# Turning the 784 tokens of two normalisations in 7 groups of 112 rows instead of 8 groups of 98

## The reference

```python
residual = x
f = _ln(x.transpose(0, 2, 3, 1), g1, b1)          # layer norm over the 96 channels
f = jnp.roll(f, (-3, -3), axis=(1, 2))
win = _window_partition(f)                        # (B * 64, 49, 96)
q, k, v = ...(win @ w_qkv + b_qkv)
attn = softmax(q @ k.T * scale + mask)            # per window and head, 49 x 49
out = (attn @ v) @ w_proj + b_proj
f = residual + roll(_window_reverse(out), (3, 3))
m = _ln(f.transpose(0, 2, 3, 1), g2, b2)          # the second layer norm
m = gelu(m @ w_fc1 + b_fc1, approximate=False) @ w_fc2 + b_fc2
return f + m.transpose(0, 3, 1, 2)
```

## Time and profile before

| what | value |
|---|---|
| median of 3 runs | 3063.34 us |
| the profiled execution, its own time | 3062.91 us |
| its span, first to last instruction | 3061.1 us |
| PE busy with matmuls | 2862.6 us, 94% |
| PE busy with weight loads (PEld, beside the matmuls) | 2299.2 us, 75% |
| DVE busy | 2424.3 us, 79% |
| ACT busy | 2076.6 us, 68% |
| POOL busy | 1454.5 us, 48% |
| mean granted TensorE clock | 0.992 |

### The profile page before, as it was taken

How to read it: one execution, slowest core, us unless ns; L and a number is a source line. 1 busy time by engine, 2 the same in 40 slices (tenths; PEclk the granted TensorE clock), 3 DMA queues, 4 the chain that set the end, 5 groups by cost and what they waited for, 6 DMA issues and landing times.

```text
span 3061.1 us, 137479 instructions
## 1 busy us (share of the span) xinstructions
PE 2862.6 (94%) x53060; PEld 2299.2 (75%) x53060; DVE 2424.3 (79%) x7208; ACT 2076.6 (68%) x3208; POOL 1454.5 (48%) x1832
## 2 busy tenths in 40 slices
PE   1799999999999999999999999999999999999997
PEld 0677777777777777777777777777777777777775
DVE  5778888788887888788787888878888788888885
ACT  0467767667776767767766767767767667777674
POOL 2554454454444444444444454444454454445444
PEclk9899999999999999999999999999999999999999
DMA  1444444444444444444444444444444444444441
GB/s 29 108 119 123 124 125 119 119 126 122 126 127 113 123 123 122 126 121 120 124 126 114 125 124 120 124 123 120 123 125 118 120 126 121 126 127 119 125 113 42
DMA packets 414727, 359.37 MB, mean 117 GB/s; under 512 B 63455, under 2 KB 413985, under 8 KB 414012
## 3 DMA queue, kind: packets, MB, share of 16 engines
q1 hardware_dynamic: 414028, 350.01, 43.7%
HBM read 193.25 MB, written 154.14 MB: 113 GB/s over the span
## 4 chain that ended last, share of the span: by engine, by line
PE 87%; issue 5%; ACT 5%; DVE 2%; POOL 1%; SPq 0%; DMA 0%; POOLq 0%; DVEq 0%; ACTq 0%
PE psum L446 18%; PE psum L379 16%; PE psum L559 11%; PE psum L430 10%; PE psum L414 8%; PE psum L472 7%; PE psum L487 6%; PE psum L532 5%; ACT probs L618 4%; PE psum L522 3%; PE psum L395 2%; PE psum L511 1%; DVE st L754 1%; POOL rs L349 0%; DVE xfl L765 0%
## 5 line engine op out<-in xcount | busy, mean ns | idle before, releaser
L618 ACT ACTIVATE probs<-psum 113x784 f32<-113x784 f32 x768 | 633.2, 824 | 652.0 <-PE psum L430 648.9
L730 DVE TENSOR_REDUCE nmax<-psum 113x16 f32<-113x784 f32 x768 | 745.3, 970 | 153.9 <-PE psum L414 153.3
L342 POOL TENSOR_SCALAR ve<-mv 98x8 f32<-98x8 f32 x264 | 64.5, 244 | 1482.4 <-DVE mv L759 1476.5
L446 PE MATMUL psum<-vbd,probs 128*49 128x18 f32 x24576 | 644.2, 198 | 9.8 <-issue 9.0
L446 PEld LDWEIGHTS psum<-vbd,probs 128*49 128x49 f32 x24576 | 634.4, 126 | 14.1 <-issue 13.3
L349 POOL TENSOR_TENSOR rs<-ve,half 98x8 f32<-98x8 f32 x264 | 440.0, 1667 | 0.0
L430 PE MATMUL psum<-qbd,kst 128*49 128x196 f16 x6144 | 405.1, 251 | 36.3 <-DVE xfl L765 23.2
L754 DVE BATCH_NORM_STATS2 st<-tok 98x6 f32<-98x96 f32 x2112 | 363.6, 245 | 84.3 <-ACT tok L625 70.8
L354 POOL TENSOR_TENSOR xn<-xn,rs 98x768 f32<-98x768 f32 x264 | 388.4, 1471 | 72.7 <-POOL rs L349 72.7
L414 PE MATMUL psum<-kbd,qst 128*49 128x196 f16 x6144 | 401.4, 250 | 7.6 <-issue 4.2
L765 DVE TENSOR_TENSOR xfl<-psum,xfh 96x784 f16<-96x784 f32 x264 | 256.0, 970 | 176.0 <-ACT xfh L630 174.2
(11 more groups left out here) (83 smaller groups left out, 5270.1 us busy)
## 6 DMA issues: line engine op xcount, KB each, us to landing
stack_pages<-nat SPq DMA_DIRECT2D x256, 294.0 KB, 3.0
kst<-stack_pages SPq DMA_DIRECT2D x256, 220.5 KB
qbd<-stack_pages SPq DMA_DIRECT2D x1024, 55.1 KB
stack_pages<-nat SPq DMA_DIRECT2D x256, 147.0 KB, 2.0
xr<-in_x_dram SPq DMA_DIRECT2D x224, 147.0 KB, 3.4
out_dram<-yr SPq DMA_DIRECT2D x224, 147.0 KB, 2.2
qst<-stack_pages SPq DMA_DIRECT2D x256, 73.5 KB
kbd<-stack_pages SPq DMA_DIRECT2D x1024, 18.4 KB
```

Of the source, the lines that this page charges most:

```text
L446: last = nc.tensor.matmul(dst[:, :, h, :], probs[:, b.c % 2, h // 4, p, h % 4 * L:(h % 4 + 1) * L], vbd[:, b.c % 4, p * NH + h, :, :], sta ...
L618: nc.scalar.activation(probs[0:PR, b.c % 2, u, :, :].rearrange("j (g q) k -> j g (q k)", g=2), psum[0:PR, B:B + 2, 0:2 * CH], ACT.Exp).the ...
L730: nc.vector.tensor_reduce(dst, psum[0:PR, A:A + 2, 0:2 * CH].rearrange("i g (q h j) -> i g q h j", q=2, j=L), axis=AX.X, op=ALU.max, negat ...
```

## The change

The two rings `xw` and `f` become one buffer `xf` in which the band's two parts of 392 tokens lie side by side, so that the 784 tokens can be cut in 7 groups of 112. `turn` does 7 transposes of 112 tokens, each into its own 128 columns of the two PSUM banks. The copy, the statistics and POOL's four steps work on 112 partitions x 7 groups. `back` uses plain float32 matmuls with the identity in place of transposes. The group that holds tokens of both parts (the fourth) is split in two matmuls of 56 columns, since the parts go to different banks. The second part of the buffer is zeroed by a memset at the start, and `turn` always does all 7 groups.

```diff
+SPAN = 112
+GROUPS = 2 * TOK // SPAN
...
-        xw = sb("xw", [C, 8, TOK])
-        tok, xn = sb("tok", [PT, 2, 2, PAIRS, C]), sb("xn", [PT, 2, 2 * PAIRS, C])
...
+        xf = sb("xf", [C, 8, 2, TOK])
+        tok, xn = sb("tok", [SPAN, 2, GROUPS, C]), sb("xn", [SPAN, 2, GROUPS, C])
...
-        f = sb("f", [C, 8, TOK])
...
+        def by_span(bank, g):
+            return psum[:, bank + g // 4, g % 4 * 128:(g % 4 + 1) * 128]
+
+        def spans(bank):
+            return psum[:, bank:bank + 2, :].rearrange("p b (g r) -> p (b g) r", g=4)[:, 0:GROUPS, :]
...  turn
-                for kind, (one, src, n) in enumerate(((b, xw, 8), (before, f, 8))):
-                    if has(one):
-                        for p in range(PAIRS):
-                            last = nc.tensor.transpose(psum[0:PT, D + kind, p * C:(p + 1) * C], src[:, one.c % n, p * PT:(p + 1) * PT], ident[0:C, 0:C])
+                both = xf[:, b.c % 8, :, :].rearrange("c k t -> c (k t)")
+                for g in range(GROUPS):
+                    last = nc.tensor.transpose(by_span(D, g)[0:SPAN, 0:C], both[:, g * SPAN:(g + 1) * SPAN], ident[0:C, 0:C])
...  back
-                for kind in range(2):
-                    for p in range(PAIRS):
-                        last = nc.tensor.transpose(psum[0:C, B + kind, p * PT:(p + 1) * PT], xn[:, b.c % 2, kind * PAIRS + p, :], ident[0:PT, 0:PT])
+                for g in range(GROUPS):
+                    first, n = divmod(g * SPAN, TOK)
+                    ends = ((0, min(SPAN, TOK - n)), (min(SPAN, TOK - n), SPAN))
+                    for kind, (lo, hi) in enumerate(ends, first):
+                        if hi > lo:
+                            at = g * SPAN + lo - kind * TOK
+                            last = nc.tensor.matmul(psum[0:C, B + kind, at:at + hi - lo], xn[:, b.c % 2, g, :], ident[0:SPAN, lo:hi], start=True, stop=True)
...  copy to tok, on ACT and on DVE
-                nc.scalar.activation(tok[:, b.c % 2, :, :, :].rearrange("t k p c -> t k (p c)"), psum[0:PT, D:D + 2, 0:PAIRS * C], ACT.Copy).then_inc(tokens_in, 1)
+                nc.scalar.activation(tok[:, b.c % 2, :, :], spans(D)[0:SPAN, :, 0:C], ACT.Copy).then_inc(tokens_in, 1)
...  first instruction of DVE
+            nc.vector.memset(xf[:, :, 1, :], 0.0)
...  statistics, and the same for bn_aggr
-                for g in range(2 * PAIRS):
-                    last = nc.vector.bn_stats(st[:, n, g, :], tok[:, n, g // PAIRS, g % PAIRS, :])
+                for g in range(GROUPS):
+                    last = nc.vector.bn_stats(st[:, n, g, :], tok[:, n, g, :])
```

More of the change, by code:

```diff
@@ L109, in build @@
         ident = sb("ident", [128, 128])
-        half = sb("half", [128, 2 * PAIRS])
+        half = sb("half", [128, GROUPS])
         wraw, w1raw = sb("wraw", [C, 3 * C]), sb("w1raw", [C, HID])
@@ L120, in build @@
         xr = sb("xr", [C, 4, WS, SIDE])
-        xw = sb("xw", [C, 8, TOK])
-        tok, xn = sb("tok", [PT, 2, 2, PAIRS, C]), sb("xn", [PT, 2, 2 * PAIRS, C])
-        st, mv = sb("st", [PT, 2, 2 * PAIRS, 6]), sb("mv", [PT, 2, 2 * PAIRS, 2])
-        ve, rs = sb("ve", [PT, 2, 2 * PAIRS]), sb("rs", [PT, 2, 2 * PAIRS])
+        xf = sb("xf", [C, 8, 2, TOK])
+        tok, xn = sb("tok", [SPAN, 2, GROUPS, C]), sb("xn", [SPAN, 2, GROUPS, C])
+        st, mv = sb("st", [SPAN, 2, GROUPS, 6]), sb("mv", [SPAN, 2, GROUPS, 2])
+        ve, rs = sb("ve", [SPAN, 2, GROUPS]), sb("rs", [SPAN, 2, GROUPS])
         xfh, xfl = sb("xfh", [FULL, 4, 2, TOK], F16), sb("xfl", [FULL, 4, 2, TOK], F16)
@@ L329, in order_x @@
                 alone(pool)
-                src, dst, inner = xr[:, b.c % 4, :, :], xw[:, b.c % 8, :], BANDS - 1
+                src, dst, inner = xr[:, b.c % 4, :, :], xf[:, b.c % 8, 0, :], BANDS - 1
                 nc.gpsimd.tensor_copy(dst[:, 0:inner * L].rearrange("c (w r s) -> c w r s", w=inner, r=WS),
@@ L338, in normalise @@
                 n = b.c % 2
-                wide_by_token = [PT, 2 * PAIRS, C]
+                wide_by_token = [SPAN, GROUPS, C]
                 pool.wait_ge(stats_done, b.count(1, 1))
@@ L344, in normalise @@
                 alone(pool)
-                nc.gpsimd.tensor_tensor(xn[:, n, :, :], tok[:, n, :, :, :].rearrange("t k p c -> t (k p) c"), mv[:, n, :, 0:1].to_broadcast(wide_by_token),
+                nc.gpsimd.tensor_tensor(xn[:, n, :, :], tok[:, n, :, :], mv[:, n, :, 0:1].to_broadcast(wide_by_token),
                                         ALU.subtract).then_inc(centred, 1)
@@ L348, in normalise @@
                 alone(pool)
-                nc.gpsimd.tensor_tensor(rs[:, n, :], ve[:, n, :], half[0:PT, :], ALU.pow).then_inc(root_done, 1)
+                nc.gpsimd.tensor_tensor(rs[:, n, :], ve[:, n, :], half[0:SPAN, :], ALU.pow).then_inc(root_done, 1)
                 pool.wait_ge(root_done, b.count(1, 1))
@@ L745, in by_token @@
                 wait(dve, normed, b.count(1, -1))
-                nc.vector.tensor_copy(tok[:, b.c % 2, :, :, :].rearrange("t k p c -> t k (p c)"), psum[0:PT, D:D + 2, 0:PAIRS * C]).then_inc(tokens_in, 1)
+                nc.vector.tensor_copy(tok[:, b.c % 2, :, :], spans(D)[0:SPAN, :, 0:C]).then_inc(tokens_in, 1)
             def stats(t):
@@ L778, in residual @@
                 wait(dve, y_made, b.count(1, -7))
-                nc.vector.scalar_tensor_tensor(out=f[:, b.c % 8, :], in0=psum[0:C, V_BANK, 0:TOK], scalar=vec[:, BP:BP + 1], in1=xw[:, b.c % 8, :],
+                nc.vector.scalar_tensor_tensor(out=xf[:, b.c % 8, 1, :], in0=psum[0:C, V_BANK, 0:TOK], scalar=vec[:, BP:BP + 1], in1=xf[:, b.c % 8, 0, :],
                                                op0=ALU.add, op1=ALU.add).then_inc(f_made, 1)
@@ L786, in result @@
                 wait(dve, y_out[back.c % 8], back.used(8, X_IN[back.c % 8])) if has(back) else None
-                dst, src, res, inner = yr[:, b.c % 2, :, :], psum[0:C, D + n, 0:TOK], f[:, b.c % 8, :], BANDS - 1
+                dst, src, res, inner = yr[:, b.c % 2, :, :], psum[0:C, D + n, 0:TOK], xf[:, b.c % 8, 1, :], BANDS - 1
                 parts = [(dst[:, :, SHIFT:SHIFT + inner * WS].rearrange("c r (w s) -> c w r s", s=WS),
```

## The result

The changed kernel takes 3258.24 us (median of 4 runs, 3254.88 to 3263.68), the kernel before 3062.85 us in the same comparison (4 runs). The ratio is 1.0641, 95% interval 1.0623 to 1.066. The forecast was 3256 us. The profiled execution of after took 3263.68 us, with a span of 3261.9; before it was 3062.91 and 3061.1.

What follows compares the result with a forecast made beforehand. PE, busy 94% of the span, was taken to bound the kernel. The terms 216 - 6.5 - 20.6 + 1 + 3 = +193 us on 3062.9 us gave 3256 us, with 3198 to 3292 us as the range for 8 in 10.

Steps and rivals of the forecast that it cites:

- Back: PE's back: plain matmuls take two loads and two passes, 1.50 us for 0.68, +0.82 per band, +216 us in all.
- The 56-column pieces: The split group in back: four records paced by their 96-column loads at 86 ns each, 0.344 us, not by 49.7 ns moving.
- Turn: PE's turn: 7 transposes for 8 save 83 ns in every two-part band, -20.6 us; one-part bands add 1 us.
- Copy, statistics, POOL: Work off PE: 0.25 us of DVE less per band and shorter POOL steps end no wait of PE's, 0 us.
- Waits: PE's gaps: the odd gap before back stays some 0.45 us and the 0.65 us slack before shifted 0 stays, 0 us.
- rival 2: Odd steps: the 0.47 us gap before back closes, so 57 us come back, 3199 us; chance 8%.
- Memset: Start of the kernel: DVE's memset of 3136 elements delays the release of the constants, +3 us (1 to 4).
- The ends of the kernel: Start and end, where PE isn't full: about half of 16 bands' longer back hides, -6.5 us.
- One pass per identity matmul: Rival for back: an identity matmul goes as one pass, back stays 0.68 us, about 3046 us; chance 5%.
- Loads that don't hide: Rival for back: no load hides behind the pass before it, +2.08 us per band, 3590 us; 5% shared with four times.
- A transpose four times cheaper: Rival for back: plain matmuls cost four times a transpose, +2.04 us per band, about 3580 us; 5% shared with unhidden loads.
- Partial cover: The longer back is partly covered in odd steps by the closing gap before it, 57 us back, 3199 us; chance 8%.

Runs made afterwards that it cites:

- before_plain: The kernel before with only back's 8 transposes of 98 columns made plain float32 matmuls against the same identity: 3223.4 us, ratio 1.0543.
- padded_transpose: As padded_plain, but back's 7 instructions are transposes of 112 columns: 3053.69 us, ratio 0.9985 to the kernel before.
- padded_plain: The kernel after with back as 7 unsplit plain matmuls at 128-column pitch, and shifted's even windows loading 64 tokens: 3227.21 us, ratio 1.0553 to the kernel before.
- before_more_stats: The kernel before with 4 more bn_stats and 4 more bn_aggr per band on DVE, into unread tiles: 3165.89 us, ratio 1.0355.
- before_long_loop: The kernel before with loop iterations of 112 steps in place of 32, the same steps in all: ratio 0.9962.
- after_long_loop: The kernel after with loop iterations of 112 steps in place of 32: ratio 1.0598 to the kernel before.

## Why the prediction was right, step by step

**Back: right in kind, 5% short in size.** Two passes and two loads per plain matmul, on the path in full: shown by before_plain, where this alone costs 166 us, and by padded_transpose, where it is gone. The 56-column pieces at the pace of their loads: forecast 86 ns, measured 85, and padded_plain confirms it by the time. The term was forecast as +0.82 us and is +0.857. The missing 0.037 is the first record of the series: 144 ns to the second in after, 48 over the steady pace, while the series of transposes in before starts with 97 ns in odd and 88 in even steps, 13 and 4 over its 84. The rule per column was fitted to series, so it could not hold the start of one.

**Turn: the mis-sized term.** Forecast 83 ns in every step, "in full, since PE's stream continues behind it". It saves 0.076 us in even steps, 0.02 of which come back behind it, and nothing in odd ones, where `expand` waits for the third exponential. So the step "in full" failed in every other step. I had read the end of `back`'s waits, but not what ends the wait at `expand`. The sum had -20.6 us there; the table gives 127 x -0.057 = -7.

**Copy, statistics, POOL at nothing:** for the direction of the change this held, since padded_transpose is no faster than its PE terms. The reason given was too generous: before_more_stats shows that the slack at shifted 0 is smaller than the two timelines suggest.

**Waits:** forecast unchanged, and 0.148 us per pair came back, 19 us. In before_plain, which has the longer `back` and no other edit, it is 1.250 - 0.722 - 0.685 = -0.157, and in padded_transpose, with the other edits and the short `back`, -0.035. So it comes with the longer `back`. 6.5 of the 19 us are the loop ends of the table above, 21.7 us before and 15.1 after. The rest is in single waits of PE, mostly in the odd step up to turn; that they get shorter because the other engines fall behind less when PE itself is slower is my reading, and no run separates them. It is no cover at the place that rival 2 named, and the forecast had no term for it.

**Memset:** +3 forecast, 3.3 to 3.5 measured. **The ends of the kernel:** +8.8 us up to the first GELU, 3.3 of them the memset. The other 5.5 are not a steady cost: between before_long_loop and after_long_loop, which differ from the two kernels only in the length of the loop, the first GELU moves by 4.2 us in all (from 164.5 to 168.6), and before_plain has it 3.7 later than before, without a memset. So of the ten longer `back`s ahead of the first GELU, 8.6 us at their full price, between 1 and 5.5 us reach the time.

**The sum** came out well since errors of both signs met: back 8 us above the forecast (127 x 1.714 = 218 for 210), turn 13 above, the start 6 above, waits 19 below. That is 8 us too much for the profiled execution, 201 for 193; the medians are 195.4 us apart. That the total came within 3 us is luck in the smaller terms; the large one, `back`, was read rightly.

**The rivals.** One pass per identity matmul is refuted by the 16 records. Loads that don't hide are refuted by 96 ns per record. A transpose four times cheaper, the rule of the Trainium skill ("TensorE: Matmul & The Clock Gate", "Terms"), is not what these kernels show: 1.39 us for 7 plain matmuls against 0.68 for 7 transposes of the same size is a factor of 2. Partial cover was 19 us and in another place than named.

## What to carry to other kernels

Count what an instruction becomes on the engine, not in the source: a float32 transpose is one load and one pass, a plain float32 matmul two of each, and an identity as operand changes nothing about that. When a regrouping cuts the number of transposes but not their moving columns, expect nothing from it on PE; in both of them the identity moves. In `turn` it has 96 columns, one for each channel, whatever the group, so one transpose fewer is 96 columns fewer; in `back` it has as many columns as the group has tokens, and their sum stays 784. Before a saving is booked, read what ends the next wait behind it in each kind of step.

## What the runs showed of the hardware beyond that

- A weight load of 96 float32 columns for a plain matmul takes 85 ns of pace and hides behind a pass of 112 columns (96 ns), but not behind one of 56 (50 ns).
- The first record of `back`'s series costs more than the later ones, and how much depends on what it is and where it stands: 48 ns in after and in padded_plain (112 columns, odd and even steps), 48 in odd and 3 in even steps of before_plain (98 columns), and for transposes 13 and 4 in before and 13 in padded_transpose.
- Shifted's load of 64 float16 columns in place of 49 costs next to nothing: the means are 109 and 103 ns in padded_transpose, its passes 252 and 251 ns, and a series of eight takes 366 ns from start to next start in place of 364.
- A loop's end costs 2 to 3 us by the times, and 1.8 to 4.0 us on average by the traces; on DVE 3.5 us pass between two instructions there, in the trace of before.
- From the end of a DVE instruction to the start of the PE instruction that waits for it 0.25 us pass in 121 even steps of before_more_stats, where PE comes to its waits while DVE is just ending, and 0.13 us at the six loop ends of before, where PE has long stood waiting.
